# The largest |h| of a 2048-column block on VectorE, in two instructions of 1024 columns in place of four of 512

## What is computed

```python
def _act_quant(x):
    scale = 127.0 / jnp.clip(jnp.max(jnp.abs(x), axis=-1, keepdims=True), 1e-05)
    return jnp.clip(jnp.round(x * scale), -128.0, 127.0) / scale

def _bitlinear(x, w):
    return jnp.einsum('bsi,oi->bso', _act_quant(x), _weight_quant(w))

def ffn(x, w_gate, w_up, w_down):                       # 512 -> 2048 -> 512
    h = jax.nn.silu(_bitlinear(x, w_gate)) * _bitlinear(x, w_up)
    return _bitlinear(h, w_down)

x = x + tanh(g_xattn) * xattn(layernorm(x), ctx, ctx, mask, ...)
x = x + tanh(g_ffn) * ffn(layernorm(x), ...)
```

## Time and profile before

| | |
|---|---|
| median of 3 runs (lowest, highest) | 1580.01 us (1579.43, 1581.88) |
| the profiled execution: its time, its span | 1580.8 us, 1579.0 us |
| mean granted clock of TensorE, share of full speed | 0.946 |
| busy TensorE | 1403.8 us (89%) |
| busy VectorE | 1056.6 us (67%) |
| busy ScalarE | 975.6 us (62%) |
| busy GpSimd | 710.6 us (45%) |
| the 256 maxima of 512 columns (L831) | 167.8 us, 676 ns each |
| chain that ended last: TensorE, VectorE, ScalarE | 73%, 8%, 6% of the span |

### The profile page before, as it was taken

The page is one execution under the profiler, slowest core; times in us unless marked ns, Lnnn a source line. Parts: engine busy times, 40 slices in busy tenths (PEclk is TensorE's granted clock), DMA queues, the critical chain, the costliest instruction groups (busy, mean ns, idle before and its releaser), DMA issues.

```text
span 1579.0 us, 29142 instructions
## 1 busy us (share of the span) xinstructions
PE 1403.8 (89%) x9088; PEld 749.3 (47%) x9408; DVE 1056.6 (67%) x2507; ACT 975.6 (62%) x1404; POOL 710.6 (45%) x1186
## 2 busy tenths in 40 slices
PE   6203579999999999999999999999999999999977
PEld 3101335545454545555554545454545555554533
DVE  5405477777778686767777777768676767776653
ACT  2303748576675848484857667584848484866644
POOL 2101226454554546363645454454636364544432
PEclk9555579999999999999999999999999999999998
DMA  5525512040403121211213040302131121303000
GB/s 201 155 24 160 162 38 76 18 117 13 115 24 112 28 86 46 85 48 53 75 39 113 13 120 13 109 18 88 46 105 46 54 72 46 86 20 87 15 14 20
DMA packets 88108, 109.09 MB, mean 69 GB/s; under 512 B 23760, under 2 KB 58416, under 8 KB 86544
## 3 DMA queue, kind: packets, MB, share of 16 engines
q1 hardware_dynamic: 88080, 108.74, 23.5%
HBM read 62.94 MB, written 37.40 MB: 64 GB/s over the span
## 4 chain that ended last, share of the span: by engine, by line
PE 73%; DVE 8%; ACT 6%; issue 5%; SPq 4%; DMA 3%; POOL 1%; ACTq 0%; DVEq 0%; POOLq 0%
PE bank L1049 21%; PE bank L1071 14%; PE bank L901 7%; PE bank L902 7%; PE bank L903 7%; PE bank L970 4%; PE bank L989 2%; SPq L338 2%; PE bank L1060 2%; PE bank L1001 2%; ACT region L608 2%; PE bank L947 2%; ACT up L596 1%; PE bank L992 1%; DVE region L825 1%
## 5 line engine op out<-in xcount | busy, mean ns | idle before, releaser
L483 POOL TENSOR_TENSOR region<-region,up 128x512 f32<-128x512 f32 x256 | 331.6, 1298 | 366.4 <-DVE region L825 217.6
L1049 PE MATMUL bank<-tern_gate,region 128*128 128x512 fp8e4 x1024 | 264.8, 381 | 13.0 <-ACT region L578 6.8
L1049 PE MATMUL bank<-tern_up,region 128*128 128x512 fp8e4 x1024 | 263.7, 380 | 0.0
L1071 PE MATMUL bank<-tern_down,region 128*128 128x512 fp8e4 x1024 | 234.1, 382 | 11.6 <-ACT region L608 11.6
L474 POOL TENSOR_TENSOR work<-work 124x512 f16<-124x512 f32 x160 | 182.7, 1156 | 97.2 <-ACT work L563 89.5
L825 DVE SCALAR_TENSOR_TENSOR region<-region,bank 128x512 f32<-128x512 f32 x256 | 171.6, 680 | 66.9 <-ACT region L588 66.2
L596 ACT ACTIVATE up<-bank 128x512 f32<-128x512 f32 x256 | 155.3, 607 | 92.8 <-PE bank L1049 92.4
L588 ACT ACTIVATE region<-bank,fs 128x512 f32<-128x512 f32 x256 | 177.1, 692 | 31.0 <-PE bank L1049 29.7
L831 DVE TENSOR_REDUCE hmx<-region 128x1 f32<-128x512 f32 x256 | 167.8, 676 | 2.5 <-POOL region L483 2.5
L600 ACT ACTIVATE region<-region,fs 128x2048 f32<-128x2048 f32 x64 | 128.5, 2008 | 54.1 <-DVE fs L842 54.1
L1049 PEld LDWEIGHTS bank<-tern_up,region 128*128 128x128 bf16 x1024 | 100.4, 98 | 121.5 <-issue 1.1
(11 more groups left out here) (148 smaller groups left out, 2620.0 us busy)
## 6 DMA issues: line engine op xcount, KB each, us to landing
q_stack<-q_rows SPq DMA_DIRECT2D x96, 256.0 KB, 4.7
xbig<-in_x SPq DMA_DIRECT2D x16, 1024.0 KB, 5.5
q_rows<-q SPq DMA_DIRECT2D x64, 256.0 KB, 2.1
out_y<-o SPq DMA_DIRECT2D x64, 256.0 KB, 2.0
q_stack<-mT SPq DMA_DIRECT2D x32, 256.0 KB, 3.9
region<-in_wgT SPq DMA_DIRECT2D x4, 1024.0 KB, 5.4
region<-in_wuT SPq DMA_DIRECT2D x4, 1024.0 KB, 7.6
region<-in_wdT SPq DMA_DIRECT2D x4, 1024.0 KB, 5.7
```

Of the source, the lines that this page charges most:

```text
L483: nc.gpsimd.tensor_tensor(ht, ht, up[:, n % 2, :], ALU.mult).then_inc(hmul_ready, 1)
L1049: ins = T.matmul(pb[2 * (n % 2) + w][:, :], xqT[:, k, tok], tern[w][:, k * FF + n * GT:k * FF + (n + 1) * GT], start=(k == 0), stop=(k == ...
L1071: ins = T.matmul(pb[2][:, :], hT[:, t % 2, k, :], tern[2][:, k * GT:(k + 1) * GT], start=(k == 0), stop=(k == FK - 1))
```

## The change

`h_amax` is called for odd blocks only. It reads the two neighbouring blocks n-1 and n as one run of 1024 columns and writes one column of `hmx`, which shrinks from 4 to 2 columns a tile. It waits for GpSimd's product of the later block, which stands behind that of the earlier one in GpSimd's order. `h_scale` waits for two maxima a tile in place of four and reduces two columns. In `VECTOR_ORDER` the words `hmt0` and `hmt2` are gone; `hmt1` and `hmt3` stay where they were among the other steps. No other engine's list changes.

```diff
--- before.py
+++ after.py
@@ -73,11 +73,9 @@
     N:xT20 F:up33 N:xT30 A:aT30 F:hq30 F:hT30 A:zq00 A:zq10 A:zq20 A:zq30
 """
 VECTOR_ORDER = """
-    A:q00 A:q10 N:ln00 A:q20 A:q30 A:s00 F:gu00 A:s01 F:gu01 A:s10 A:s11 F:hm00 A:s20 A:s21 F:gu02 F:gu03 F:hm01
-    A:s30 A:s31 F:gu10 A:mh00 F:hm02 F:hm03 F:hs00 F:gu11 F:gu12 N:xn00 F:gu13 F:hm10 F:down00 F:hm11 F:hm12
-    F:gu20 N:xn10 F:hm13 F:hs10 A:pv00 F:gu21 A:pv01 F:hm20 F:gu22 A:pv02 F:gu23 A:pv03 F:hm21 A:aT00 F:down10
-    A:aT10 F:hm22 F:hm23 A:pv10 F:hs20 F:gu30 A:pv11 N:xn20 F:gu31 N:xT00 A:pv12 A:pv13 F:gu32 N:xn30 F:hm30
-    F:gu33 N:xT10 A:aT20 F:hm31 F:hm32 A:aT30 F:hm33 N:xT20 N:xT30 F:hs30 F:down20 A:wo00 A:st00 A:wo10 A:st10
+    A:q00 A:q10 N:ln00 A:q20 A:q30 A:s00 F:gu00 A:s01 F:gu01 A:s10 A:s11 A:s20 A:s21 F:gu02 F:gu03 F:hm01
+    A:s30 A:s31 F:gu10 A:mh00 F:hm03 F:hs00 F:gu11 F:gu12 N:xn00 F:gu13 F:down00 F:hm11     F:gu20 N:xn10 F:hm13 F:hs10 A:pv00 F:gu21 A:pv01 F:gu22 A:pv02 F:gu23 A:pv03 F:hm21 A:aT00 F:down10
+    A:aT10 F:hm23 A:pv10 F:hs20 F:gu30 A:pv11 N:xn20 F:gu31 N:xT00 A:pv12 A:pv13 F:gu32 N:xn30     F:gu33 N:xT10 A:aT20 F:hm31 A:aT30 F:hm33 N:xT20 N:xT30 F:hs30 F:down20 A:wo00 A:st00 A:wo10 A:st10
     A:wo20 A:zn00 A:zn10 A:st20 A:za00 F:down30 A:za10 A:wo30 A:st30 A:zn20 A:za20 A:zn30 A:za30
 """
 POOL_ORDER = """
@@ -196,7 +194,7 @@
         rcp = sb("rcp", [P, 2, HH], f32)
         fs = sb("fs", [P, TT, 16], f32)
         AMAX, AQ, SQ, AQ2, CG, KAP, HMX, HCL, HAQ, HRC, HSC, HOUT = range(12)
-        hmx = sb("hmx", [P, 2, FN], f32)
+        hmx = sb("hmx", [P, 2, FN // 2], f32)
         lnc = sb("lnc", [P, 3, TT], f32)
 
         pb = [ctx.enter_context(nc.psum_tensor(f"bank{i}", [P, 512], f32)) for i in range(8)]
@@ -826,14 +824,14 @@
 
             def h_amax(f, t, n):
 
-                ht = h[:, t % 2, n * GT:(n + 1) * GT]
+                pair = h[:, t % 2, (n - 1) * GT:(n + 1) * GT]
                 dve.wait_ge(hmul_ready, f * (TT * FN) + (t * FN + n + 1))
-                V.tensor_reduce(hmx[:, t % 2, n:n + 1], ht, AX.X, ALU.max, apply_absolute_value=True).then_inc(hmax_ready, 1)
+                V.tensor_reduce(hmx[:, t % 2, n // 2:n // 2 + 1], pair, AX.X, ALU.max, apply_absolute_value=True).then_inc(hmax_ready, 1)
 
             def h_scale(f, t, _):
                 at = lambda i: fs[:, t, i:i + 1]
                 dve.wait_ge(ffn_scalars, f * (2 * TT) + (2 * t + 2))
-                dve.wait_ge(hmax_ready, f * (TT * FN) + (t * FN + FN))
+                dve.wait_ge(hmax_ready, f * (TT * FN // 2) + (t + 1) * (FN // 2))
                 done = f * (4 * TT) + 4 * t
                 fstep(V.tensor_reduce(at(HMX), hmx[:, t % 2, :], AX.X, ALU.max), done + 1)
                 fstep(V.tensor_scalar(at(HCL), at(HMX), at(KAP), EPS, ALU.mult, ALU.max), done + 2)
```

## The result

The changed kernel takes 1616.24 us (median; 1614.81 to 1617.03), the kernel before 1580.16 us beside it. The ratio is 1.0226, interval 1.0208 to 1.0243: 36 us slower, where 5.6 us were forecast and 1590.5 was the upper end.

The account below looks back on a forecast made before the run. TensorE was taken to bound the loop (busy 98.87 of 100 us). 14 turns of +0.33 us gave +4.6, the tail +1.0: +5.6 on 1580.0, so 1585.6 us, range 1578.5 to 1590.5.

Parts of the forecast that it names:

- the rule for the place: VectorE's order: each pair's first maximum leaves its slot (0.594 us earlier behind it), the second becomes 0.537 us longer.
- Tile 0: hm00 to down00: gu11 and hs00 about 0.1 us later, yet -0.08 us a turn at down00; bounds -0.40 and +0.15.
- Tile 1: Behind gu20: hm13 0.537 us longer makes pv00's normalisation late, so pv01 costs +0.45 us a turn; bounds 0.25 to 0.60.
- price rule: Late normalisation, read from pv13: pv01 would start at 696.55, and gu23 at 697.21 in place of 696.75.
- Tile 2: hm20 and hm21 lie ahead of waits: zero; neighbours hm22 and hm23 give -0.06 us, lost in the next TensorE wait.
- Tile 3: hm30's removal ends the wait ahead of aT30, but ScalarE's copies hold down20: -0.04 us a turn, bounds 0 and -0.54.
- the rival that the freed slots pay: At down20: VectorE's chain holds it, so hm30's removal returns about 0.5 us a turn; 1579.2 us, chance 20%.
- The tail: FFN alone: hs10's quantisation +0.50 us later, hm33's 0.537 us counts in full; together +1.0 us.
- The last overlapped turn: Turn without xn10: pv01 has 0.61 us to spare, costs at most 0.05 us, about what its own -0.08 gives back.
- The clock rival: In the tail: 0.5 us longer waits bring another down block to the lower clock, +2.3 us; 1587.9 us, chance 5%.
- The price of the edit: One 1024-column maximum takes 1.213 us against 1.270 for two in a row; bounds 1.14 to 1.35.
- VectorE's sum: Sign in the profile after: VectorE's sum lower by 10 to 18 us.

Follow-up runs that it names:

- both_fixes: Changed kernel with `mh` one place earlier in VectorE's order and the last two scale steps reading one operand through a scalar pointer: 1597.50 us.
- mh_first: Changed kernel with mh00 moved ahead of gu10 in VectorE's order, nothing else: 1599.63 us.
- adjacent: Kernel before, with wide maxima only where two narrow ones are neighbours (hm02+hm03, hm11+hm12, hm22+hm23): 1584.84 us.
- fused: Kernel before, narrow maxima kept, scale steps of h cut from six to four ahead of the next gate product: 1577.46 us, ratio 0.9981.

## Why the prediction was wrong

**The failing step** is the rule for the place: the second maximum "becomes 1.213-0.676 = 0.537 us longer" and "everything behind it is 0.537 later". It moves VectorE's steps by fractions of a microsecond and keeps every duration. Two of those behind the wide maxima aren't constants: the second step of `mh` went from 0.225 to 1.284 us and hs10's scale from 0.16 to 0.80, because they now start behind a GpSimd product and not ahead of it. The distance to that point was 0.06 us at `mh` and 0.16 at hs10's scale (695.15 against 695.31), both less than the shifts that the prediction itself worked out (0.537-0.25-0.15 = 0.14 us at `mh`, 0.537 at hs10). The sum has no term at the transposes of `mhl` at all, where the hold costs 0.87 us a turn, and in no rival does a step behind the maxima change its duration, so the measured time lies above all of them. The turn's 2.44 us, counted on TensorE from one set of transposes of `mhl` to the next (turns compared: 85.22 and 87.66 us long):

| place | forecast | after | both_fixes |
|---|---|---|---|
| transposes of `mhl`, end of the turn | 0 | +0.87 | 0 |
| ahead of them (ScalarE's xq30, hm00 gone) | in tile 0 | -0.17 | -0.17 |
| tile 0, to down00 | -0.08 | +0.36 | +0.42 |
| tile 1, to pv01 | +0.45 | +1.08 | +0.55 |
| tile 2, to pv13 | 0 | +0.30 | +0.41 |
| tile 3, to down20 | -0.04 | 0 | 0 |
| sum | +0.33 | +2.44 | +1.21 |

**Tile 0.** "gu11 and the scale step hs00 come about 0.1 us later" failed twice. The 1.06 us hold of `mh` (1284-225 ns) was not seen at all. And without it (`mh_first`) gu13 still waits 0.77 us: gu11 comes 0.25 us later against TensorE's xq30. Taking hm00 away made hm01 only 0.20 us earlier (forecast 0.25) and the wait ahead of gu10 was 0.06 (forecast 0.15), while TensorE's own products come 0.17 earlier. Down00 is 0.31 later behind the transposes in `mh_first`, with the -0.17 ahead of them +0.14: the upper bound, not the -0.08 taken.

**Tile 1.** Place, mechanism and price rule held: 0.39 us of wait and +0.55 at pv01 without the hold, inside the bounds of 0.25 to 0.60. The term was mis-sized by the hold of the scale, 1.08-0.55 = 0.53.

**Tile 2.** "hm22 and hm23 are neighbours: -0.06" took the wide instruction to be ready when the first narrow one is. It has the readiness of the later block, and the layer-norm step behind it, held by GpSimd, passes the delay on to pv13: +0.30 a turn, shown in `adjacent`, where tiles 0 and 1 cost nothing.

**Tile 3.** Right. In the changed kernel the wait ahead of aT30 is gone, and down20 waits for ScalarE's copies of hT20, as said for the earlier trace rows:

```profile
645.93 1.94 ACT L606 ACTIVATE region<-bank 128x1024 bf16<-128x1024 int16 x2
...
647.01 0.60 PE L999 MATMUL bank<-ident,at 128*128 128x128 f32 x4
...
648.03 1.25 PE L1069 MATMUL bank<-tern_down,region 128*128 128x512 fp8e4 x5 [0.42 <-ACT region L606]
```

So the rival that the freed slots pay is refuted: 0.24 us of wait for VectorE became 0.42 for ScalarE.

**The tail** came out as forecast. ScalarE's quantisations after (first and last two of four; the last is tile 3's):

```profile
1565.00 1.99 ACT L598 ACTIVATE region<-region,fs 128x2048 f32<-128x2048 f32 x1
1579.52 2.00 ACT L598 ACTIVATE region<-region,fs 128x2048 f32<-128x2048 f32 x1 [0.40 <-DVE fs L840]
1592.85 2.00 ACT L598 ACTIVATE region<-region,fs 128x2048 f32<-128x2048 f32 x1
1603.15 2.00 ACT L598 ACTIVATE region<-region,fs 128x2048 f32<-128x2048 f32 x1 [3.78 <-DVE fs L840]
```

and before (the second of the four is in the earlier trace rows):

```profile
1527.90 1.99 ACT L600 ACTIVATE region<-region,fs 128x2048 f32<-128x2048 f32 x1
...
1555.21 2.00 ACT L600 ACTIVATE region<-region,fs 128x2048 f32<-128x2048 f32 x1
1564.98 2.00 ACT L600 ACTIVATE region<-region,fs 128x2048 f32<-128x2048 f32 x1 [3.25 <-DVE fs L842]
```

From the first to the second it is 14.52 us where it was 14.02, from the third to the fourth 10.30 where it was 9.77: +0.50 for hs10 and +0.53 for hm33, forecast 0.50 and 0.54.

**The last overlapped turn** was forecast at about nothing. Of the +1.60 between the 14 turns and the first quantisation of the tail, 0.46 lie in it. The other 1.15 arise between the second and third gate products of the tail, at the clock: behind a wait of TensorE of 6.8 us in both kernels, the granted clock was 0.50 and 0.86 in the two stretches of 5 us from 1510 before, 0.50 and 0.53 in those from 1545 after. The lower of the two levels stayed longer.

**The clock rival** went the other way at the very end. The last down block took 5.91 us before and 3.63 after, and that is the -2.27 of the account. After, the block ahead of it took the longer time:

```profile
1598.97 5.31 PE L1069 MATMUL bank<-tern_down,region 128*128 128x512 fp8e4 x16 [1.62 <-ACT region L606]
1607.90 3.63 PE L1069 MATMUL bank<-tern_down,region 128*128 128x512 fp8e4 x16 [1.62 <-ACT region L606]
```

There it cost nothing at the end, since TensorE still waited 0.92 us for ScalarE behind it (2.08 before). The time from the last quantisation to the end, 11.7 to 14.6 us in the 14 profiled executions, moves with this, as much as some of the differences in the table; the 14 turns, all at a granted clock of 1.00, don't have this.

**The price of the edit** (1.213 us a pair) was right, at 1.210. What the prediction says of the Trainium skill beside it ("VectorE: DVE Perf Modes", "The DRAIN you can't avoid") leaves out the end of that paragraph, by which a next operation that isn't held back starts earlier; the 0.594 us of the earlier trace rows agree with it. VectorE's sum, forecast 10 to 18 us lower, rose: its busy time by 18.4, of which 15.9 and 9.0 are the two held instructions, against 12.9 less for the maxima. This sum alone said that durations had changed.

## What to carry to other kernels

Before a VectorE step is moved by a fraction of a microsecond, list the instructions behind it that read two SBUF tensors, or that show two durations in the trace, as the layer-norm step with one tensor does here, and the GpSimd instructions beside them: if one starts just ahead of a GpSimd instruction, the cost of moving it is the rest of that instruction and not the move. A merged instruction is ready when its last input is, so a merge of two neighbours can cost the wait that the first one used to fill. Instructions that are small, stand at such an edge and are waited for go first; with one element a partition, reading one operand as a pointer scalar helped as well.

## What the hardware showed that was not expected

The hold doesn't depend on the size of the instruction: the scale with one element a partition was held 0.64 us (0.80 in place of 0.16), the 128x64 step 1.06 us; each ended within 0.1 us of the end of GpSimd's instruction. The pointer form of the one-element step costs 213 ns in place of 159 and isn't held. GpSimd gives way too: in the kernel before, its product takes 1.51 us in place of 1.27 to 1.30 when VectorE's layer-norm step started 0.16 us ahead of it.

```profile
693.08 0.54 DVE L751 TENSOR_SCALAR xn<-xbig,mv,rs 128x512 f32 x1
...
693.24 1.51 POOL L483 TENSOR_TENSOR region<-region,up 128x512 f32<-128x512 f32 x1
```

This layer-norm step reads one tensor and two pointer scalars, so one tensor input alone doesn't keep an instruction free. It lasted 0.54 us here and 1.12 us at 680.42, 0.43 us behind the start of a product at 679.99. Where it starts well inside a product, it ends 0.28 us behind the product's end wherever it starts: it takes 1.15 us when it starts 0.41 behind the product's start (`adjacent`), 0.95 at 0.60 (before), 0.75 at 0.81 (`fused`). The sign was in the trace of before: one instruction of one size with two durations.

TensorE's granted clock in 14 us near the end, in stretches of 5, 5 and 4 us, was 0.76, 0.56 and 0.85 before (from 1565) and 0.75, 1.00 and 1.00 after (from 1600). The low stretch came earlier, and the last block ran at the upper of the two levels.
